# Softmax division of the second attention by 32 by 32 transposes, and the output projection issued one place earlier

## The chip, the cores and the metric

The kernel runs on one core of one Trainium2 chip. A core has TensorE (PE, matrix products), VectorE (DVE), ScalarE (ACT), GpSimd (POOL) and SyncE (SP, which only issues DMAs); each has a queue of its own that it works through in order, and they wait for each other by semaphores. Matrix products are written to PSUM (eight banks of 512 float32 columns on 128 partitions), the rest lives in SBUF. The metric is the device time in microseconds of one execution.

## The reference, cut to what matters

Two layers, each `x + attention(norm(x)) * silu(ffn(norm(x)))`, on 32 batches of 256 tokens with 128 channels (16 heads of 8). The change lies in the second layer's attention:

```python
q, k, v = xn @ q_w, xn @ k_w, xn @ v_w          # 16 heads of 8
scores = q @ k.T / sqrt(8)                      # q times sigmoid(unity_scale)
allowed = (j % 4 == 0) | (abs(i - j) <= 8)      # 64 strided keys and a band
attn = softmax(where(allowed, scores, -inf))
out = (attn @ v) @ o_w + o_b
x = x + out * silu(moe(xn))                     # 8 experts, top 2, capacity 2048
```

## The kernel before

The kernel goes through five stages: norm and projections, first attention with routing, first experts, end of layer 1, then the second attention with the second experts in its midst. The second attention works one batch of 256 tokens a step; `t` counts the steps in every engine's program. After step `MOE_AFTER` = 21 all engines run the second layer's experts, and steps 22 to 32 follow. From step 23 on, the steps also hold the final sums (`combine_last`, `gate_last` on VectorE, `tanh_last` on ScalarE, `sum_last` on GpSimd, loads and stores on SyncE), one group of 512 tokens in about every 0.6 steps.

The order of the work is written out by hand, in a loop over `t` in each engine's program. TensorE's step `t` is, in order:

1. first half of the maxima of batch t+1 (`maxima_pe`, lines 1779 and 1783: scores with queries on partitions, in banks 0 to 3),
2. weighing of the values, second half of the heads of batch t-1 (`weigh`, line 1845, into bank 6),
3. scores of batch t, first half of the heads (`second_scores`, line 1816) and the maximum subtracted (`less_maximum`, line 1826), banks 2 to 5,
4. keys of batch t+2 (`keys_second`, line 1743, bank 7),
5. second half of the maxima of batch t+1,
6. output projection of batch t-1 (`output_second`, line 1854, four products into bank 6),
7. values of batch t+1 (`values_second`, line 1753, bank 7),
8. weighing, first half of the heads of batch t; scores, second half; the maximum turned (`turn_max`, line 1799), queries of batch t+3 (line 1728).

The second half of the maxima writes banks that ScalarE's exponential (`exponents`, line 883) has to read first: it waits for the first of the two instructions of `exponents(t, 0)`. The first reduction of the maxima has to be done before the scores of the same half are written.

VectorE's step `t`: both reductions of the first maxima (`maxima_dve`, line 1355, 1024 columns each), the division of batch t-1 (`divide_second`), in late steps final sums (lines 1407, 1410, 1420), the result taken out of bank 6 with the bias added (`keep_second`, line 1396, which waits for the output projection), both reductions of the second maxima, and the maximum split into three bf16 parts (`split_max`, lines 1366 to 1372). TensorE's next weighing into bank 6 (item 8) waits for line 1396.

ScalarE's step: in the old kernel the masked copy `second_halves` (line 892) of bank 6, the exponentials, copies and masks of keys, queries and values.

What the division does: bank 6 holds, on the 32 partitions of each of four groups of heads, for heads 0 and 1 of the group the values on rows 0 to 15 and the sums of the exponentials on rows 16 to 31 (columns 0 to 255 are the queries), and for heads 2 and 3 (columns 256 to 511) the other way round. Before, the two column halves were mixed into DEN and NUM by two masks over partitions, with ScalarE's copy SEC of the masked half, DEN was moved by 16 partitions (`stream_shuffle`), inverted (256 columns) and multiplied with NUM.

The division of batch 21 and its projection lie in the experts' stage, behind the first transpose of rows and the first up-projection; the last division is at the very end, behind the last group's sums.

Of the kernel before, what the change touches and what calls it, by code (L numbers as in the profile page):

```python
# [8 lines left out]
ALU = mybir.AluOpType  # L9
# [3 lines left out]
P = 128  # L13
T = 8192
NT = T // P
NB = 32
# [149 lines left out]
def memory(nc, ctx, a, out):  # L166
# [50 lines left out]
    m.tix = small[:, 72:144]  # L217
    m.pcol = small[:, 144:145]
    m.eoff = small[:, 146:154]
    m.first_half, m.second_half = small[:, 158:159], small[:, 159:160]  # L220
    m.row = small[:, 160:302]
    m.mk = [small[:, 154 + j:155 + j] for j in range(4)]
    lg_words = m.LG[:].rearrange("p i e -> p (i e)")
# [105 lines left out]
    m.KS.append(sbx(bt, "KS2", [P, 576]))  # L329
    m.K4.append(sbx(bt, "K41", [P, 4, 320]))  # L330
    m.Q4.append(sbx(bt, "Q41", [P, 4, 256]))
    m.RC = sbx(bt, "RC", [P, 256])
    m.YC = sbx(bt, "YC", [P, 256])
    r.O = sbx(bt, "r1O", [P, 2, NT, E], BF16)
    r.O2 = r.O[:].rearrange("p k i e -> p (k i) e")
# [12 lines left out]
    x.W = [sbx(bt, f"W1_{k}", [P, 2, 512]) for k in range(2)]  # L348
    x.X = [sbx(bt, f"X1_{k}", [P, 2 * ROW]) for k in range(6)]
    m.b1s, m.b2s = sbx(bt, "b1s", [P, E, 4]), sbx(bt, "b2s", [P, E, C])  # L350
    m.SEC = sbx(bt, "SEC", [P, 512])
    m.DEN, m.NUM = sbx(bt, "DEN", [P, 256]), sbx(bt, "NUM", [P, 256])
    bt.close()

    xn_words = m.XNp[:].rearrange("p i c -> p (i c)")
# [28 lines left out]
def semaphores(nc, ctx):  # L384
    s = Sems()

    def sem(name):
        return ctx.enter_context(nc.semaphore(name))

    s.v_seq = sem("v_seq")  # L390

    s.const, s.upb, s.sw, s.zero, s.w0, s.c1, s.bb = (sem("l_" + n) for n in ("const", "upb", "sw", "zero", "w0", "c1", "bb"))
    s.zero_y, s.placed, s.to, s.nb, s.norm_a, s.norm_p, s.cnt_row = (sem(n) for n in (
        "l_zero_y", "placed", "to", "nb", "norm_a", "norm_p", "cnt_row"))

    s.wv0, s.vl, s.va, s.vd = (sem(n) for n in ("l_wv0", "vl", "va", "vd"))
    s.x = [sem(f"l_x{k}") for k in range(8)]
    s.scat0, s.scat1 = sem("l_scat0"), sem("l_scat1")

    s.zero_ready, s.var, s.rstd, s.norm, s.xpose, s.xt = (sem(n) for n in (  # L400
        "zero_ready", "var", "rstd", "norm", "xpose", "xt"))

    s.gate, s.gate_exp, s.onehot, s.cnt, s.cnt_sb, s.rank, s.total, s.total_sb, s.low, s.low_used, s.slots, s.ub = (
        sem(n) for n in ("gate", "gate_exp", "onehot", "cnt", "cnt_sb", "rank", "total", "total_sb", "low", "low_used",
                         "slots", "ub"))

    s.zvm, s.proj, s.rt, s.rq, s.ka, s.qm, s.vm, s.sc1, s.ev1, s.mask, s.sc2, s.prod, s.pv, s.yt = (sem(n) for n in (
        "zvm", "proj", "rt", "rq", "ka", "qm", "vm", "sc1", "ev1", "mask", "sc2", "prod", "pv", "yt"))

    s.at_row, s.xg, s.eup, s.eact, s.edown, s.y = (sem(n) for n in ("l_at_row", "xg", "eup", "eact", "edown", "y"))  # L410
    s.W = [[sem(f"l_W{n}_{k}") for k in range((5, 2)[n])] for n in range(2)]
    s.X = [[sem(f"l_X{n}_{k}") for k in range(6)] for n in range(2)]
    s.Y = [[sem(f"l_Y{n}_{k}") for k in range(4)] for n in range(2)]

    s.sup, s.hact, s.sdown = (sem(n) for n in ("sup", "hact", "sdown"))
    s.xb = [sem(f"l_xb{k}") for k in range(5)]
    s.yg = [sem(f"l_yg{k}") for k in range(3)]
    s.x1d = [sem(f"l_x1d{k}") for k in range(5)]
    s.comb, s.u, s.tanh, s.oproj, s.p6, s.x1, s.lg1, s.lg_sb = (sem(n) for n in (
        "comb", "u", "tanh", "oproj", "p6", "x1", "lg1", "lg_sb"))  # L420

    s.zw, s.zv, s.xw, s.qp, s.kp, s.vp, s.qs, s.ks, s.vn, s.q4, s.k4 = (sem(n) for n in (
        "zw", "zv", "xw", "qp", "kp", "vp", "qs", "ks", "vn", "q4", "k4"))
    s.scl_a, s.scl, s.max, s.maxv, s.neg, s.mturn, s.mvt = (sem(n) for n in (
        "scl_a", "scl", "max", "maxv", "neg", "mturn", "mvt"))
    s.sc, s.ex, s.wv, s.sec, s.yn, s.o1, s.given = (sem(n) for n in ("sc", "ex", "wv", "sec", "yn", "o1", "given"))
    s.zg = [sem(f"l_zg{k}") for k in range(NF)]
    s.zx = [sem(f"l_zx{k}") for k in range(NF)]
    s.out = [sem(f"l_out{k}") for k in range(NF)]
    s.fcomb, s.ftanh, s.taken, s.fex, s.fx = (sem(n) for n in ("fcomb", "ftanh", "taken", "fex", "fx"))  # L430
    return s
# [452 lines left out]
                     m.ps[:, (2 + 2 * half) * 512:(4 + 2 * half) * 512], ACT.Exp, scale=m.scl[:, 0:1]).then_inc(s.ex, 1)  # L884


def second_halves(e, m, s, b):

    e.wait_ge(s.wv, 2 * b + 2)
    if b >= 1:  # L890
        e.wait_ge(s.yn, b)
    e.mul(m.SEC[:], m.PS[6][:, 0:512], m.second_half).then_inc(s.sec, 1)


def expert_act(e, m, s, x, n, func, bias):
    if n == 0:
        e.wait_ge(s.ub, 1)
# [45 lines left out]
def scalar_program(e, m, s):  # L943
# [82 lines left out]
    for t in range(NB + 1):  # L1026
        if t == 2:
            e.wait_ge(s.gate, 2)
            e.activation(m.LG[:], m.LG[:], ACT.Exp).then_inc(s.gate_exp, 1)
        if t < 2:  # L1030
            end_act(e, m, s, NG - 2 + t, 1)
        if 1 <= t < NB and t - 1 != MOE_AFTER:
            second_halves(e, m, s, t - 1)
        if t < NB:
            exponents(e, m, s, t, 0)
        if t < 2:
            end_act(e, m, s, NG - 2 + t, 2)
        if t + 2 < NB:
            keys_copy(e, m, s, t + 2)
            keys_apart(e, m, s, t + 2)  # L1040
        if t + 1 < NB:
            value_pad(e, m, s, t + 1)
        for p in pairs_combined(t)[0]:
            tanh_last(e, m, s, p)
        if t + 1 < NB:
            queries_apart(e, m, s, t + 1, (0, 1))
        if t < NB:
            exponents(e, m, s, t, 1)
        if t + 1 < NB:
            queries_apart(e, m, s, t + 1, (2, 3))  # L1050
            maximum_copy(e, m, s, t + 1)
        if t + 3 < NB:
            queries_copy(e, m, s, t + 3)
        for p in pairs_combined(t)[1]:
            tanh_last(e, m, s, p)
        if t == NB:
            second_halves(e, m, s, NB - 1)
        if t == MOE_AFTER:
            second_halves(e, m, s, t)
            expert_act(e, m, s, m.x1, 1, ACT.Relu, lambda i, j: m.b1s[:, i // 8, j:j + 1])  # L1060


# [311 lines left out]

def divide_second(e, m, s, o, b):

    first, second = m.PS[6][:, 0:256], m.PS[6][:, 256:512]
    e.wait_ge(s.sec, b + 1)
    den = o.mark(e.scalar_tensor_tensor(m.DEN[:], second, m.first_half, m.SEC[:, 0:256], ALU.mult, ALU.add))
    o.mark(e.scalar_tensor_tensor(m.NUM[:], first, m.first_half, m.SEC[:, 256:512], ALU.mult, ALU.add))  # L1380
    o.wait(den)
    o.mark(e.stream_shuffle(m.RC[:], m.DEN[:], [i ^ 16 for i in range(32)]))
    o.wait()
    o.mark(e.reciprocal(m.RC[:], m.RC[:]))
    o.wait()
    if b >= 1:
        e.wait_ge(s.o1, b)
    e.tensor_tensor(m.YC[:], m.NUM[:], m.RC[:], ALU.mult).then_inc(s.yn, 1)


def keep_second(e, m, s, b):
# [559 lines left out]
def tensor_program(e, m, s):  # L1951
# [79 lines left out]
    for t in range(NB + 1):  # L2031
        if t == 0:
            turn_max(e, m, s, 0)
        if t + 1 < NB and t != MOE_AFTER + 1:
            maxima_pe(e, m, s, t + 1, 0)
        if t == MOE_AFTER + 1:
            e.wait_ge(s.y, NX0 + NX1)
        if t >= 1 and t - 1 != MOE_AFTER:
            weigh(e, m, s, t - 1, 1)
        if t in (0, 1, 6):  # L2040
            e.wait_ge(s.mvt, t + 1)
            e.wait_ge(s.qs, t + 3)
        if t < 2:
            end_pe(e, m, s, NG - 2 + t, 1)
        if t == 6:
            route_ranks(e, m, s, m.r1, 1, 0)
        if t < NB:
            second_scores(e, m, s, t, 0)
            less_maximum(e, m, s, t, 0)
        if t < 2:  # L2050
            end_pe(e, m, s, NG - 2 + t, 2)
        if t + 2 < NB:
            keys_second(e, m, s, t + 2)
        if t + 1 < NB:
            maxima_pe(e, m, s, t + 1, 1)
        if t >= 1 and t - 1 != MOE_AFTER:
            output_second(e, m, s, t - 1)
        if t + 1 < NB:
            values_second(e, m, s, t + 1)
        if t < NB:  # L2060
            weigh(e, m, s, t, 0)
            if t in (5, 6):
                e.wait_ge(s.vn, t + 2)
            if t == 5:
                route_counts(e, m, s, m.r1, 1)
            if t == 6:
                route_ranks(e, m, s, m.r1, 1, 1)
            second_scores(e, m, s, t, 1)
            less_maximum(e, m, s, t, 1)
        if t + 1 < NB:  # L2070
            turn_max(e, m, s, t + 1)
        if t + 3 < NB:
            queries_second(e, m, s, t + 3)
        if t == MOE_AFTER:
            weigh(e, m, s, t, 1)
            e.wait_ge(s.maxv, 4 * t + 8)
            e.wait_ge(s.ex, 4 * t + 4)
            expert_pe(e, m, s, m.x1, 1)
# [27 lines left out]
def _constants():  # L2106
# [11 lines left out]
    sm[:, 160:302] = np.arange(P)[:, None] + P * np.arange(142)[None, :]  # L2118
    for j in range(4):
        sm[:, 154 + j] = (np.arange(P) // 8) % 4 == j  # L2120
    sm[:, 158] = (np.arange(P) // 16) % 2 == 0
    sm[:, 159] = (np.arange(P) // 16) % 2 == 1
    c["c_small"] = sm
    c["c_tok"] = np.tile(NX1 * SL + np.arange(2 * NT, dtype=f) * P, (P, 1)).astype(f)
    inv = (f(1.0) / np.power(f(10000.0), np.arange(0, 8, 2, dtype=f) / f(8))).astype(f)
# [78 lines left out]
```

## Time and profile before

| | us |
|---|---|
| median of 3 runs | 1639.22 (1637.23 to 1644.84) |
| the profiled execution | 1639.27 |
| its span, first to last instruction | 1638.0 |
| mean granted TensorE clock | 0.991 of full speed |
| second attention, steps 0 to 21 | 950 to 1248 |
| second attention, steps 22 to 32 | 1478 to 1638 |

Busy time is counted per engine over the whole span. The chain of waits is followed back from the last instruction, at each step to what released it. In the timelines a number in brackets is the time that the engine idled before the row, with the engine and line that ended it; PEld is TensorE's weight load, which runs beside its products.

### The profile page before, as it was taken

How to read it: one execution, taken by the hardware profiler on the slowest of the kernel's cores; microseconds unless marked ns; L12 is line 12 of the kernel's file. 1: busy time of each engine (PE TensorE's matmuls, PEld its weight loads, DVE VectorE, ACT ScalarE, POOL GpSimd, SP SyncE). 2: the span in 40 equal slices, each digit the busy share in tenths (PEclk: the TensorE clock that was granted, in tenths of full speed). 3: DMA queues.
4: the chain of work that ended last, by engine and by line, in shares of the span. 5: the costliest groups of instructions: out<-in, count | busy, mean ns of one | idle time of the engine just before them, and what ended most of it. 6: DMA issues, size and time to landing. Idle time of an engine off the chain costs nothing.

```text
span 1638.0 us, 46884 instructions
## 1 busy us (share of the span) xinstructions
PE 1523.8 (93%) x18055; PEld 1110.6 (68%) x18059; DVE 1025.1 (63%) x2095; ACT 1007.8 (62%) x2071; POOL 830.5 (51%) x908
## 2 busy tenths in 40 slices
PE   7999999999999999999999989899998999999884
PEld 5555444555545889988777756666666999996553
DVE  6788898878775222212499969877775222226997
ACT  5767666777765444544545557777776455456773
POOL 7334587888874455545212210377774555552432
PEclk9999999999999999999999989999999999999998
DMA  9910002000004889888344310011113544433434
GB/s 313 417 56 1 8 31 100 29 28 30 30 29 85 229 216 245 230 216 235 91 117 120 85 55 3 16 50 44 47 45 60 95 89 101 90 70 97 117 100 117
DMA packets 296954, 169.45 MB, mean 103 GB/s; under 512 B 198080, under 2 KB 273216, under 8 KB 293792
## 3 DMA queue, kind: packets, MB, share of 16 engines
q1 hardware_dynamic: 277312, 128.45, 30.1%
q0 software_dynamic: 16832, 34.64, 6.1%
q10 hardware_dynamic: 2592, 3.38, 0.7%
q8 instruction: 147, 2.41, 0.6%
q14 instruction: 71, 0.58, 0.1%
HBM read 96.74 MB, written 69.63 MB: 102 GB/s over the span
## 4 chain that ended last, share of the span: by engine, by line
PE 59%; DVE 12%; issue 9%; POOL 9%; DMA 4%; ACT 4%; SPq 3%; DVEq 0%; POOLq 0%; ACTq 0%
PE ps L1884 12%; PE ps L1875 12%; PE ps L1688 6%; POOL xd L624 4%; DVE s_RS L1355 4%; PE ps L1916 4%; POOL s_S L657 4%; PE ps L1904 3%; PE ps L1779 3%; DMA s_W<-in_ew 3%; PE ps L1816 3%; ACT s_PX L883 3%; PE ps L1712 3%; PE ps L1652 2%; SPq L461 2%
## 5 line engine op out<-in xcount | busy, mean ns | idle before, releaser
L817 ACT ACTIVATE s_S<-ps 128x512 f32<-128x512 f32 x384 | 208.4, 595 | 141.4 <-PE ps L1688 141.4
L624 POOL DMA_INDIRECT xd<-s_XN,s_slots x256 | 251.2, 981 | 84.8 <-issue 62.2
L1542 DVE TENSOR_TENSOR s_PP<-ps,s_S 128x1024 f32<-128x1024 f32 x192 | 234.4, 1221 | 74.2 <-PE ps L1688 52.7
L1688 PE MATMUL ps<-s_QM,s_KK 32*128 32x512 f32 x1536 | 233.8, 639 | 2.7 <-ACT s_S L817 2.7
L906 ACT ACTIVATE s_HH<-ps,s_LG 128x256 f32<-128x256 f32 x284 | 125.2, 474 | 138.1 <-PE ps L1875 135.5
L641 POOL DMA_INDIRECT yd<-s_Y,s_to x142 | 136.0, 958 | 138.4 <-DVE s_Y L1484 114.3
L657 POOL TENSOR_SCALAR_AFFINE_SELECT s_S<-s_S 128x1024 f32<-128x1024 f32 x128 | 140.6, 1098 | 114.3 <-ACT s_S L817 113.7
L1355 DVE TENSOR_REDUCE s_RS<-ps 128x8 f32<-128x1024 f32 x128 | 150.3, 1216 | 62.0 <-PE ps L1783 62.0
L883 ACT ACTIVATE s_PX<-ps,s_scl 128x1024 f32<-128x1024 f32 x128 | 135.7, 1111 | 86.8 <-PE ps L1826 86.8
L906 ACT ACTIVATE s_XN<-ps,s_b1s 128x256 f32<-128x256 f32 x256 | 113.3, 474 | 113.9 <-PE ps L1875 110.6
L641 POOL DMA_INDIRECT yd<-s_XN,s_to x128 | 122.5, 957 | 117.0 <-DVE s_XN L1484 95.1
L1484 DVE TENSOR_TENSOR s_Y<-ps,s_W 128x256 f32<-128x256 f32 x71 | 30.1, 424 | 210.3 <-PE ps L1884 210.3
L1875 PE MATMUL ps<-s_XG,s_W 128*128 128x256 f32 x568 | 136.8, 384 | 13.3 <-DMA s_W<-in_ew 12.5
L1884 PEld LDWEIGHTS ps<-s_W,s_HH 128*128 128x128 f32 x1136 | 137.8, 192 | 3.6
L1884 PE MATMUL ps<-s_W,s_HH 128*128 128x128 f32 x1136 | 138.1, 275 | 0.0
L1484 DVE TENSOR_TENSOR s_XN<-ps,s_b2s 128x256 f32<-128x256 f32 x64 | 27.2, 424 | 171.5 <-PE ps L1884 171.5
L1712 PEld LDWEIGHTS ps<-s_PP,s_VM 128*32 128x32 f32 x3072 | 76.1, 109 | 84.8 <-DVE s_PP L1542 52.1
L1884 PEld LDWEIGHTS ps<-s_W,s_XN 128*128 128x128 f32 x1024 | 124.3, 192 | 3.3
L1875 PE MATMUL ps<-s_XN,s_W 128*128 128x256 f32 x512 | 122.9, 383 | 3.9 <-DVE s_XN L1471 3.0
L1884 PE MATMUL ps<-s_W,s_XN 128*128 128x128 f32 x1024 | 124.6, 275 | 0.0
L1875 PEld LDWEIGHTS ps<-s_XG,s_W 128*128 128x128 f32 x568 | 102.3, 190 | 28.2 <-DMA s_W<-in_ew 15.4
L795 ACT ACTIVATE s_QM<-s_RQ,s_small 128x256 f32<-128x256 f32 x252 | 113.9, 507 | 0.4 <-issue 0.4
(223 smaller groups left out, 2782.8 us busy)
## 6 DMA issues: line engine op xcount, KB each, us to landing
s_W<-in_ew SPq DMA_DIRECT2D x71, 576.0 KB, 4.6
s_X<-xd SPq DMA_DIRECT2D x540, 32.0 KB
xd<-s_zero SPq DMA_DIRECT2D x16, 1056.0 KB, 18.1
s_YG<-yd SPq DMA_DIRECT2D x32, 256.0 KB, 3.7
s_XN<-yd SPq DMA_DIRECT2D x32, 256.0 KB, 4.0
yd<-s_zero SPq DMA_DIRECT2D x7, 1056.0 KB, 27.9
s_XN<-in_x SPq DMA_DIRECT2D x8, 512.0 KB, 7.1
xd<-s_XN,s_slots POOLq DMA_INDIRECT x256
```

The costliest lines, as they stand in the source:

```text
L624: e.indirect_dma_start(out=xd, out_offset=bass.IndirectOffsetOnAxis(ap=m.slots[:, k, i:i + 1], axis=0), in_=m.XNp[:, i, 0:C + 1], in_offse ...
L641: e.indirect_dma_start(out=x.yd, out_offset=bass.IndirectOffsetOnAxis(ap=m.to[n][:, 2 * i + t:2 * i + t + 1], axis=0), in_=x.Y[i % 4][:, t ...
L657: e.affine_select(out=sel, in_=sel, pattern=[[0, 8], [1, P]], compare_op=ALU.is_ge, fill=0.0, base=0, channel_multiplier=-1).then_inc(s.ma ...
L817: e.mul(m.S1[u % 3][:, t * 512:(t + 1) * 512], m.PA[:, t * 512:(t + 1) * 512], 1.0 / 64.0).then_inc(s.ev1, 1)
L883: e.activation(m.PX[hp][:, 2 * half:2 * half + 2, :].rearrange("p r n -> p (r n)"), m.ps[:, (2 + 2 * half) * 512:(4 + 2 * half) * 512], AC ...
L906: e.activation(x.HH[i % 2][:, j, :], m.PS[j][:, 0:SL], func, bias=bias(i, j)).then_inc(s.eact, 1)
L1355: e.tensor_reduce(m.MM[b % 2][:, hf, 8 * rp:8 * rp + 8], m.ps[:, 1024 * rp:1024 * rp + 1024].rearrange("p (x n) -> p x n", x=8), AX.X, ALU ...
L1542: e.tensor_tensor(m.PP[u % 4][:], m.PB[u % 2], m.S1[u % 3][:], ALU.mult).then_inc(s.prod, 1)
L1688: return e.matmul(out, m.KK[k][32 * r:32 * r + 32, kind, kc * P:(kc + 1) * P], m.QM[k][32 * r:32 * r + 32, kind, :, qc * P:(qc + 1) * P], ...
L1712: i = e.matmul(m.PS[6][32 * c:32 * c + 32, qc * P:(qc + 1) * P], m.VM[b % 2][:, kc, 4 * c + h, :], m.PP[(2 * q + c // 2) % 4][:, (c % 2) * ...
L1875: e.matmul(PS[j][:, 0:SL], W[:, 0, j * P:(j + 1) * P], x.XG[i % 2][:], start=True, stop=True).then_inc(s.eup, 1)
L1884: ins = e.matmul(PS[4 + i % 2][:, c * P:(c + 1) * P], x.HH[i % 2][:, j, c * P:(c + 1) * P], W[:, 1, j * C:(j + 1) * C], start=(j == 0), st ...
```

## The change

VectorE transposes bank 6 (512 columns) in squares of 32 by 32 into TM, so that 32 queries lie on the partitions of a group and each head's sum is one column for 32 queries. It inverts 32 columns, multiplies twice (128 columns each, the inverse repeated 8 times) into YM and transposes YM (256 columns) back into YC. It waits for the weighing itself (`wv`) where it waited for ScalarE's copy (`sec`). The copy, its semaphore, the tensors SEC, DEN and NUM and the two masks are gone; the tensors are placed anew, RC has 32 columns. On TensorE `output_second(t - 1)` stands in front of `maxima_pe(t + 1, 1)`; in step 21's experts and in its own waits it is unchanged.

```diff
 def divide_second(e, m, s, o, b):
 
-    first, second = m.PS[6][:, 0:256], m.PS[6][:, 256:512]
-    e.wait_ge(s.sec, b + 1)
-    den = o.mark(e.scalar_tensor_tensor(m.DEN[:], second, m.first_half, m.SEC[:, 0:256], ALU.mult, ALU.add))
-    o.mark(e.scalar_tensor_tensor(m.NUM[:], first, m.first_half, m.SEC[:, 256:512], ALU.mult, ALU.add))
-    o.wait(den)
-    o.mark(e.stream_shuffle(m.RC[:], m.DEN[:], [i ^ 16 for i in range(32)]))
-    o.wait()
-    o.mark(e.reciprocal(m.RC[:], m.RC[:]))
-    o.wait()
+    e.wait_ge(s.wv, 2 * b + 2)
+    o.mark(e.transpose(m.TM[:], m.PS[6]))
+    o.wait()
+    o.mark(e.reciprocal(m.RC[:].rearrange("p (b h x) -> p b h x", b=8, h=2), view(m.TM[:], 16, [[32, 8], [240, 2], [8, 2]])))
+    o.wait()
+    for hp in range(2):
+        value = view(m.TM[:], 272 * hp, [[32, 8], [8, 2], [1, 8]])
+        one_over = view(m.RC[:], 2 * hp, [[4, 8], [1, 2], [0, 8]])
+        o.mark(e.tensor_tensor(view(m.YM[:], 16 * hp, [[32, 8], [8, 2], [1, 8]]), value, one_over, ALU.mult))
+    o.wait()
     if b >= 1:
         e.wait_ge(s.o1, b)
-    e.tensor_tensor(m.YC[:], m.NUM[:], m.RC[:], ALU.mult).then_inc(s.yn, 1)
+    e.transpose(m.YC[:], m.YM[:]).then_inc(s.yn, 1)
...
-def second_halves(e, m, s, b):
-
-    e.wait_ge(s.wv, 2 * b + 2)
-    if b >= 1:
-        e.wait_ge(s.yn, b)
-    e.mul(m.SEC[:], m.PS[6][:, 0:512], m.second_half).then_inc(s.sec, 1)
...
@@ scalar_program
-        if 1 <= t < NB and t - 1 != MOE_AFTER:
-            second_halves(e, m, s, t - 1)
...
-        if t == NB:
-            second_halves(e, m, s, NB - 1)
         if t == MOE_AFTER:
-            second_halves(e, m, s, t)
...
@@ tensor_program
             keys_second(e, m, s, t + 2)
+        if t >= 1 and t - 1 != MOE_AFTER:
+            output_second(e, m, s, t - 1)
         if t + 1 < NB:
             maxima_pe(e, m, s, t + 1, 1)
-        if t >= 1 and t - 1 != MOE_AFTER:
-            output_second(e, m, s, t - 1)
```

## Rows read from the trace of the kernel before

**Rows 1.** The page's busy time of each engine, share of the span, instructions.

```profile
PE 1523.8 (93%) x18055; PEld 1110.6 (68%) x18059; DVE 1025.1 (63%) x2095; ACT 1007.8 (62%) x2071; POOL 830.5 (51%) x908
```

**Rows 2.** Pieces of the chain of waits, steps 10, 11 and 15: start, us, what.

```profile
1094.27 1.12 ACT s_PX L883
...
1104.14 1.24 DVE s_RS L1355
...
1163.38 2.35 DVE s_RS L1355 x2
```

**Rows 3.** Timeline of step 10: start, us, engine, line, operation, shapes [idle before].

```profile
1089.55 1.12 PE L1779 MATMUL ps<-s_K,s_QS 32*64 32x512 f32 x16 [0.31 <-ACT s_PX L883]
...
1091.03 2.35 DVE L1355 TENSOR_REDUCE s_RS<-ps 128x8 f32<-128x1024 f32 x2 [2.62 <-PE ps L1783]
...
1093.33 0.48 DVE L1379 SCALAR_TENSOR_TENSOR s_DEN<-ps,s_small,s_SEC 128x256 f32<-128x256 f32 x1
...
1094.51 0.70 PE L1743 MATMUL ps<-s_XW,s_RS 128*128 128x320 f32 x2
...
1095.44 1.12 PE L1779 MATMUL ps<-s_K,s_QS 32*64 32x512 f32 x16 [0.23 <-ACT s_PX L883]
...
1096.38 0.43 DVE L1388 TENSOR_TENSOR s_YC<-s_NUM,s_RC 128x256 f32<-128x256 f32 x1
...
1096.93 0.64 PE L1854 MATMUL ps<-s_RS,s_YC 128*128 128x128 f32 x4
...
1097.41 1.06 PE L1753 MATMUL ps<-s_RS,s_XW 128*128 128x128 f32 x8
1097.61 0.42 DVE L1396 TENSOR_TENSOR s_RS<-ps,s_RS 128x256 f32<-128x256 f32 x1 [0.80 <-PE ps L1854]
1097.96 1.21 DVE L1355 TENSOR_REDUCE s_RS<-ps 128x8 f32<-128x1024 f32 x1
```

**Rows 4.** Durations by line on VectorE, ns: min/median/max, first and last start.

```profile
L1384 DVE RECIPROCAL s_RC<-s_RC x32: 1752/1753/1754, 971.3 to 1631.3; 128x256 f32<-128x256 f32 x32
...
L1246 DVE RECIPROCAL s_mx<-s_mx x1: 553/553/553, 993.0 to 993.0; 128x64 f32<-128x64 f32 x1
...
L1471 DVE STREAM_TRANSPOSE s_XN<-s_X x64: 403/434/446, 1250.7 to 1471.3; 128x256 f32<-128x256 f32 x64
...
L1447 DVE TENSOR_TENSOR s_XN<-s_XN x1: 691/691/691, 1629.4 to 1629.4; 128x512 f32<-128x512 f32 x1
...
L1368 DVE TENSOR_TENSOR s_RS<-s_RS x32: 191/193/633, 946.9 to 1606.7; 128x32 f32<-128x32 f32 x32
```

**Rows 5.** Waits, 950 to 1250 us: total us, times, longest.

```profile
PE ps L1816 <- DVE s_RS L1355: 8.1, 21, 1.3
...
PE ps L1799 <- DVE s_RS L1372: 1.2, 3, 0.5
```

**Rows 6.** Who waited for line 1355, 1055 to 1240 us: total us, times.

```profile
  PE ps L1816: 3.7, 14
```

**Rows 7.** Timeline of TensorE in step 24.

```profile
1515.91 1.10 PE L1845 MATMUL ps<-s_PX,s_VN 128*32 128x64 f32 x64 [1.25 <-DVE s_RS L1396]
```

**Rows 8.** Who waited for line 1396, whole span: total us, times.

```profile
  PE ps L1845: 8.8, 9
```

**Rows 9.** Chain of waits, first reductions of steps 23 and 30, first and last of eight.

```profile
1493.35 2.35 DVE s_RS L1355 x2
...
1595.75 2.27 DVE s_RS L1355 x2
```

**Rows 10.** Timeline of step 31 and the end.

```profile
1609.49 1.10 PE L1845 MATMUL ps<-s_PX,s_VN 128*32 128x64 f32 x64 [1.66 <-ACT s_PX L883]
...
1611.38 0.48 DVE L1379 SCALAR_TENSOR_TENSOR s_DEN<-ps,s_small,s_SEC 128x256 f32<-128x256 f32 x1 [3.46 <-ACT s_SEC L892]
...
1622.16 3.91 DVE L1407 TENSOR_SCALAR s_XN<-s_XN,s_wgt 128x128 f32<-128x128 f32 x4
...
1633.55 1.22 PE L1854 MATMUL ps<-s_RS,s_YC 128*128 128x128 f32 x4 [9.69 <-DVE s_YC L1388]
```

More of the change, by code:

```diff
@@ L219, in memory @@
     m.eoff = small[:, 146:154]
-    m.first_half, m.second_half = small[:, 158:159], small[:, 159:160]
     m.row = small[:, 160:302]
@@ L331, in memory @@
     m.Q4.append(sbx(bt, "Q41", [P, 4, 256]))
-    m.RC = sbx(bt, "RC", [P, 256])
+    m.YM = sbx(bt, "YM", [P, 256])
     m.YC = sbx(bt, "YC", [P, 256])
@@ L350, in memory @@
     m.b1s, m.b2s = sbx(bt, "b1s", [P, E, 4]), sbx(bt, "b2s", [P, E, C])
-    m.SEC = sbx(bt, "SEC", [P, 512])
-    m.DEN, m.NUM = sbx(bt, "DEN", [P, 256]), sbx(bt, "NUM", [P, 256])
+    m.TM = sbx(bt, "TM", [P, 512])
+    m.RC = sbx(bt, "RC", [P, 32])
     bt.close()
@@ L425, in semaphores @@
         "scl_a", "scl", "max", "maxv", "neg", "mturn", "mvt"))
-    s.sc, s.ex, s.wv, s.sec, s.yn, s.o1, s.given = (sem(n) for n in ("sc", "ex", "wv", "sec", "yn", "o1", "given"))
+    s.sc, s.ex, s.wv, s.yn, s.o1, s.given = (sem(n) for n in ("sc", "ex", "wv", "yn", "o1", "given"))
     s.zg = [sem(f"l_zg{k}") for k in range(NF)]
@@ L2120, in _constants @@
         sm[:, 154 + j] = (np.arange(P) // 8) % 4 == j
-    sm[:, 158] = (np.arange(P) // 16) % 2 == 0
-    sm[:, 159] = (np.arange(P) // 16) % 2 == 1
     c["c_small"] = sm
```

## The prediction

> **What bounds the kernel now.** I read the busy table first: TensorE works 93% of the span, VectorE 63% [rows 1], so VectorE's saved time is worth something only where it ends a wait. The diff touches the second attention, 32 batches: steps 0 to 21 lie at 950 to 1248 us, steps 22 to 32 at 1478 to 1638 us, the second experts between. I then read the chain of waits there. In a usual step it runs through TensorE, with ScalarE's first exponential as one link: 1094.27 + 1.12 ends at X = 1095.39, and TensorE goes on 0.05 later [rows 2]. VectorE stands in it for one reduction. Steps 1 to 21 each hold an output projection. In 8 of these 21 the chain passes through both reductions of the second group (2.35 us together [rows 2]), so VectorE's queue sets the pace. The other 13 are TensorE's. I call them V-steps (8) and T-steps (13).
>
> The timeline of one T-step [rows 3] shows where the division lies. VectorE's reductions end at R = 1093.38; five instructions follow, from 1093.33 to 1096.81 (the last starts at 1096.38, 0.43 long): 3.48 us. TensorE meanwhile does the keys (to 1095.21), waits 0.23 for X, does the second maxima from 1095.44, the output projection from 1096.93, the values from 1097.41. The division is done before its consumer's turn. VectorE then waits 0.80 us for the projection before line 1396, and only after that reduces the second group, at 1097.96 = X + 2.57.
>
> **The division, step by step.** Reciprocal costs 1.753 us for 256 columns and 0.553 for 64 [rows 4], 6.25 ns a column, so 32 columns take 0.553 - 0.200 = 0.35. A transpose of 256 columns takes 0.434, an elementwise one of 256 0.42 [rows 3, 4], of 512 0.69, of 32 0.19 [rows 4], about 1.04 ns a column over 0.16. So the transpose of 512 is 0.70, the two products of 128 columns are 0.29 each, and the second starts some 0.08 before the first ends, as lines 1379 and 1380 overlap in the trace (0.50 for both), the last transpose 0.43. With three hand-overs of 0.04: 0.70 + 0.04 + 0.35 + 0.04 + 0.50 + 0.04 + 0.43 = 2.10, against 3.48: 1.38 less.
> No row shows a transpose of 512 columns out of PSUM. Below it cannot be under 0.43 (256 columns), above I take the 1.21 of a reduction of 1024 PSUM columns [rows 3]. The reciprocal of 32 lies between 0.19 (another operation of 32) and 0.55, the products between 0.19 and 0.42 each. Together the chain is between 1.6 and 3.2; I take 2.10, since the nearest rows lie on one line.
> The Trainium skill, "VectorE: DVE Perf Modes", section on the TRN2 errata, adds 62 cycles at 0.96 GHz to an operation whose source is in PSUM. The trace has 0.42 for line 1396 (PSUM) and 0.43 for line 1388 (SBUF) [rows 3], so it does not bear this out. By the rule the chain would be 2.16 and the estimate below some 2 us higher.
>
> **ScalarE's masked copy** (L892) leaves, 0.69 us in each batch. It was hidden: in the steps it runs while VectorE reduces and ends before R. It counted only in step 31, where VectorE waited 3.46 for it [rows 10]: the weighing there ends at 1610.59, the division starts at 1611.38, 0.79 later; 0.05 will do, so 0.74 goes.
>
> **The projection in front.** It now stands behind the keys and waits for the division; the second maxima, values, weighing and scores queue behind it. The division ends at 1093.33 + 2.10 = 1095.43, or X + 0.04. Then 0.05 of latency, 0.1 for a weight load that nothing hides now, and 0.46 for its four products: the maxima start at X + 0.65 instead of X + 0.05. The maxima need 1.49 until the next operation starts (1095.44 to 1096.93), so the values start at X + 2.14 instead of 1097.41 = X + 2.02. With the cold start of the maxima I take 0.15 of loss in a T-step. If the division ended before 1095.2 the projection would lie wholly in the hole and a T-step would gain up to 0.2.
> In T-steps: 13 x 0.15 = 1.95 us slower.
> In V-steps the reductions no longer wait for the projection and line 1396. They start when the first maxima banks are done, 1.48 after the maxima begin (1089.55 to 1091.03 in the other half of this step), at X + 2.13 instead of X + 2.57: 0.4 earlier on VectorE's side, 0.15 later on TensorE's [rows 3]. What can be won is how long TensorE waited more than in a T-step. It waited 8.1 us in 21 waits for the first reduction [rows 5] where 3.7 us in 14 are usual (0.264 each) [rows 6], so 2.5 over, and 1.2 for the split maximum [rows 5]: 3.7 in 8 steps. Each gives back at most 0.4, less the 0.15: some 1.8 in all.
> The two cancel: steps 1 to 21 come out at 0, and the experts' stage too, where the projection stands behind the first up-projection and the division fits beside it.
>
> **Steps 23 to 30.** Here VectorE also does the final sums, ahead of line 1396. Step 24 shows it: the weighing behind line 1396 starts at 1515.91 after 1.25 us of idle TensorE [rows 7]; nine such waits make 8.8 us [rows 8]. The division sits in front of all that, so its 1.38 comes off directly until TensorE is the limit again: a T-step lasts 13.1 (first reductions at 1091.03 [rows 3] and 1104.14 [rows 2]; over the T-steps the mean is 13.05), with the loss 13.2 us. The first reductions of the eight steps start between 1493.35 and 1595.7 [rows 9]; the seven steps between them are 13.90, 15.04, 14.76, 13.91, 14.68, 13.90 and 16.13 us. The three near 13.9 fall to 13.2 (0.70 each), the four others by 1.38, and the last by 1.3: 2.1 + 5.5 + 1.3 = 8.9 us.
>
> **Step 31 and the end.** In step 31 the masked copy and the division lie open: 0.74 + 1.38 = 2.1. VectorE's queue is then unbroken from line 1396 to the last division, with one slow group (3.91 us for four instructions [rows 10]). The last division starts at 1630.03, long after its weighing, and the projection waits for it until 1633.55 [rows 10]: 1.4 more.
>
> Sum: 0 + 8.9 + 2.1 + 1.4 = 12.4 us. The profiled execution took 1639.27 us (span 1638.0), within 0.1 of the median, so the forecast is 1627.
>
> **Rivals.** With the chain at 2.10 + d, about 31 places pay d (21 steps, 8 in the tail, 2 at the end), so the time is 1627 + 31 d and no gain is left at d = 0.40.
> A, slower: the projection blocks TensorE's queue. If the transpose out of PSUM needs twice the 0.70, d is 0.7, the maxima start at X + 1.35 in every step, and the sum is -12.4 + 21.7 = +9.3: 1648.6. For it: nothing in the trace shows this operation, and the wait is new. Against: all VectorE rows on PSUM go at the pace of those on SBUF. Chance 0.10.
> B, little gain: in the tail VectorE and GpSimd get in each other's way. Four instructions of line 1407 took 3.91 us beside GpSimd's sums, and 0.87 elsewhere, 3.0 more [rows 10]. If moving the queue makes two more such meetings, or TensorE takes more than 0.15 for the new order (0.3 in 28 steps costs 4 more), the time is 1632 to 1635. Chance 0.20. The Trainium skill, "SBUF — State Buffer", section "SBUF: two separate sides", calls the port pair of the two engines an exclusive lock that also VectorE instructions with two SBUF inputs ask for; the new products are such, as the old one was.
> C, more gain: the division is 0.25 shorter, the projection falls into the hole behind the keys. T-steps then give 0.2 instead of taking 0.15 (13 x 0.35 = 4.6), V-steps and tail some 3: 1620. Chance 0.13.
> My forecast, 1622 to 1631: 0.55. The remaining 0.02 is for what I have not seen.
>
> **Range and chances.** The bounds of the chain give 1616 (d = -0.5, where the hole caps the gain) to 1660 (d = 1.1); 80% is 1619 to 1639. What a measurement here can tell from no change is about 0.5%, 8.2 us: under 1631 counts as faster, over 1647.4 as slower. Faster 0.71 (forecast, C, a little of B), same 0.20, slower 0.09.
>
> **What would show it.** The division from its first transpose to its last: 2.1 us, the first 0.70, the reciprocal 0.35. The projection starts about 0.05 after the last transpose and within 0.2 of X. TensorE's wait for line 1396 goes from 8.8 us to under 1. T-steps stay within 0.3 of 13.05. Steps 23 to 30 shrink by 0.7 to 1.4 each. A projection that waits more than 0.5 behind the keys, or T-steps above 13.4, would make the prediction wrong; so would tail steps that don't shrink.

## The result, and the profile after

The changed kernel takes 1637.87 us (median of 20 runs, 1632.88 to 1642.11); the kernel before, run beside it, 1642.21 us (20 runs). The ratio is 0.9972 with a 95% interval of 0.9962 to 0.9983: faster by 0.28%, 4 to 5 us, where 12.4 us were forecast. That lies within the 0.5% that the prediction takes for no change, and outside its 1622 to 1631.

The page's busy row of the changed kernel, as [rows 1]:

```profile
PE 1530.1 (94%) x18055; PEld 1116.5 (68%) x18059; DVE 986.2 (60%) x2063; ACT 986.5 (60%) x2039; POOL 832.0 (51%) x908
```

VectorE gave up 38.9 us, ScalarE 21.3 us (32 masked copies), and the span shrank by 2.1 us (1635.9 after 1638.0). TensorE does the same 18055 instructions and is busy 6.3 us longer. That says little by itself, since its mean granted clock was 0.988 here and 0.991 before.

The timeline of step 9 of the new kernel around its division, first VectorE, then TensorE, to be read against [rows 3] (start, us, engine, line, operation; in brackets the idle time before and what ended it):

```profile
1080.33 2.36 DVE L1341 TENSOR_REDUCE s_RS<-ps 128x8 f32<-128x1024 f32 x2 [3.50 <-PE ps L1770]
1082.61 0.70 DVE L1364 STREAM_TRANSPOSE s_TM<-ps 128x512 f32<-128x512 f32 x1
1083.34 0.35 DVE L1366 RECIPROCAL s_RC<-s_TM 128x32 f32<-128x32 f32 x1
1083.73 0.49 DVE L1371 TENSOR_TENSOR s_YM<-s_TM,s_RC 128x128 f32<-128x128 f32 x2
1084.26 0.45 DVE L1375 STREAM_TRANSPOSE s_YC<-s_YM 128x256 f32<-128x256 f32 x1
1085.51 0.42 DVE L1383 TENSOR_TENSOR s_RS<-ps,s_RS 128x256 f32<-128x256 f32 x1 [0.80 <-PE ps L1841]
1086.88 2.36 DVE L1341 TENSOR_REDUCE s_RS<-ps 128x8 f32<-128x1024 f32 x2 [0.94 <-PE ps L1770]
```

```profile
1083.81 0.70 PE L1730 MATMUL ps<-s_XW,s_RS 128*128 128x320 f32 x2
1084.76 0.71 PE L1841 MATMUL ps<-s_RS,s_YC 128*128 128x128 f32 x4 [0.25 <-DVE s_YC L1375]
1085.40 1.11 PE L1766 MATMUL ps<-s_K,s_QS 32*64 32x512 f32 x16
1086.45 0.61 PE L1770 MATMUL ps<-s_RS,s_identb 128*128 128x256 bf16 x4
1086.89 1.06 PE L1740 MATMUL ps<-s_RS,s_XW 128*128 128x128 f32 x8
1087.88 1.20 PE L1832 MATMUL ps<-s_PX,s_VN 128*32 128x64 f32 x64
1089.01 0.72 PE L1803 MATMUL ps<-s_Q,s_KS 32*128 32x128 f32 x14
1090.14 0.93 PE L1803 MATMUL ps<-s_Q,s_KS 32*128 32x128 f32 x18 [0.41 <-issue]
1091.01 1.05 PE L1813 MATMUL ps<-s_RS,s_AUG 128*128 128x256 bf16 x8
```

The division runs from 1082.61 to 1084.71: 2.10 us, as forecast. The projection starts 0.05 later and the second maxima 0.64 after it. In the last row but one TensorE stops for 0.41 in the middle of its 32 score products, and no semaphore ends that. The bracket understates it: from the first score product to the next group it takes 2.00 us (1089.01 to 1091.01), in a step without a stop 1.11. The kernel before has no such stop of over 0.15 us in its second attention.

The wait of [rows 8] in the new kernel (who waited for line 1383, whole span: total us, times), and the new kernel's rows of step 31 and the end, as [rows 10]:

```profile
  PE ps L1832: 0.2, 1
```

```profile
1610.63 1.10 PE L1832 MATMUL ps<-s_PX,s_VN 128*32 128x64 f32 x64 [1.66 <-ACT s_PX L882]
...
1611.80 0.72 DVE L1364 STREAM_TRANSPOSE s_TM<-ps 128x512 f32<-128x512 f32 x1 [2.74 <-PE ps L1832]
...
1621.70 3.61 DVE L1394 TENSOR_SCALAR s_XN<-s_XN,s_wgt 128x128 f32<-128x128 f32 x4 [0.22 <-DMA s_XN<-yd]
...
1631.42 1.22 PE L1841 MATMUL ps<-s_RS,s_YC 128*128 128x128 f32 x4 [7.78 <-DVE s_YC L1375]
```

To see where the gain went I measured distances between the starts of the maxima groups on TensorE (line 1779 before, 1766 after). Half a step lies between two of them. Two halves are one step. An ordinary step is the length of the steps that nothing else disturbs. "Steps 2-21" runs from the first maxima of step 2 to the second maxima of step 21, "experts" from there to the first maxima of step 22, "steps 22-29" from there to those of step 30. For all kernels of one chip, in us, from their profiled executions:

| kernel | ordinary step | steps 2-21 | experts | steps 22-29 | the rest |
|---|---|---|---|---|---|
| before | 13.02 | 258.7 | 238.4 | 114.7 | 45.5 |
| changed | 13.19 | 263.8 | 238.9 | 110.5 | 40.6 |
| division only (e1) | 12.97 | 257.7 | 239.3 | 108.1 | 40.7 |
| move only (e2) | 14.56 | 289.6 | 238.0 | 118.6 | 47.6 |
| division between (e3) | 12.78 | 259.8 | 238.5 | 112.6 | 41.4 |

"The rest" runs from step 30 to the end of the span. The changed kernel wins 9.1 us in the last two columns and loses 5.1 in steps 2 to 21; 1.8 more are lost at the beginning and in the experts, of which 1.1 lie ahead of the second attention. Of the 5.1, 0.7 is the measuring point: the second maxima of step 21 now stand behind the projection. From the first maxima of step 2 to those of step 21 the loss is 4.5 us.

The time up to step 2 isn't in the table. It is 980.8, 982.1, 987.7, 981.1 and 988.2 us in the order of the rows. The profiled execution of e1 took 4.8 us more than the median of its kernel, that of e3 3.2 more, and it is in this part that they are long. So the columns are compared one by one, and whole times by medians.

### The profile page after: what moved, and what is told of

It reads as the page before. It is cut to its first block, busy times and chain, and to the rows that moved or that the text cites. A ratio compares the mean times of both kernels' runs of the same rounds, so it can differ in the third digit from the quotient of the medians.

```text
span 1635.9 us, 46789 instructions
## 1 busy us (share of the span) xinstructions
PE 1530.1 (94%) x18055; PEld 1116.5 (68%) x18059; DVE 986.2 (60%) x2063; ACT 986.5 (60%) x2039; POOL 832.0 (51%) x908
## 4 chain that ended last, share of the span: by engine, by line
PE 62%; DVE 11%; POOL 9%; issue 8%; DMA 4%; ACT 3%; SPq 2%; POOLq 0%; DVEq 0%; ACTq 0%
PE ps L1871 13%; PE ps L1862 13%; PE ps L1675 6%; DVE s_RS L1341 4%; POOL xd L623 4%; PE ps L1766 4%; POOL s_S L656 4%; PE ps L1903 4%; PE ps L1891 3%; PE ps L1699 3%; PE ps L1639 2%; DMA s_W<-in_ew 2%; PE ps L1803 2%; PE ps L1832 2%; ACT s_PX L882 2%
## 5 line engine op out<-in xcount | busy, mean ns | idle before, releaser
L897 ACT ACTIVATE s_XN<-ps,s_b1s 128x256 f32<-128x256 f32 x256 | 113.3, 474 | 115.4 <-PE ps L1862 111.2
```

Of the source, the lines that this page charges most:

```text
L897: e.activation(x.HH[i % 2][:, j, :], m.PS[j][:, 0:SL], func, bias=bias(i, j)).then_inc(s.eact, 1)
```

## The experiments

**The changed kernel again (e0).** No edit. 

> The changed kernel once more, nothing altered. Theory O (order): the projection in front of the second maxima costs 0.2 us in every step where TensorE sets the pace, so such a step lasts 13.2 to 13.25 us again (before: 13.05). Theory S (stalls): in the first trace TensorE stood still seven times for 0.2 to 0.9 us in the midst of a row of equal products, with nothing waited for (3.1 us in all, none in the kernel before); if these belong to the new order they come back at about the same places, if they are an accident of the execution they come back elsewhere or not at all. Time as measured, 0.996 to 0.999 of the kernel before.

Measured: 1638.37 us, ratio 0.9975 (0.9961 to 0.999). TensorE's stops, told of below, come back in the same steps (at 998.10, 1081.57, 1095.08, 1188.96, 1559.75, 1586.44 and 1592.64 us, and a small one at 1101.78), though this execution runs some 5 us later. They belong to the program and not to chance, though two of them differ in length (0.17 and 0.76 in the first execution, 0.72 and 0.22 here).

**The division alone (e1).** TensorE in its old order:

```diff
-        if t >= 1 and t - 1 != MOE_AFTER:
-            output_second(e, m, s, t - 1)
         if t + 1 < NB:
             maxima_pe(e, m, s, t + 1, 1)
+        if t >= 1 and t - 1 != MOE_AFTER:
+            output_second(e, m, s, t - 1)
```

> The new division with the projection left behind the second maxima. Theory O: steps 1 to 21 go at 13.05 us again, the steps 23 to 30 fall as far as 13.05 instead of 13.2, the end gains the same 4.8 us (masked copy and two open divisions): 9 to 14 us under the kernel before, 5 us or more under the changed kernel. Rival, stalls alone (S as an accident): the order costs nothing, this kernel is within 2 us of the changed one, and its ordinary steps are no shorter. Rival, the prediction's V-steps: the earlier projection was worth 1.8 us in the eight steps that VectorE paces, which this kernel gives up, so those steps are as long as before.

Measured: 1629.96 us, ratio 0.9917 (0.9901 to 0.9934), 13.9 us under the kernel before and 8.4 under the changed one. It beats both. Its timeline of TensorE in a usual step:

```profile
1087.68 0.70 PE L1730 MATMUL ps<-s_XW,s_RS 128*128 128x320 f32 x2
1088.61 1.12 PE L1766 MATMUL ps<-s_K,s_QS 32*64 32x512 f32 x16 [0.23 <-ACT s_PX L882]
...
1090.11 0.61 PE L1841 MATMUL ps<-s_RS,s_YC 128*128 128x128 f32 x4
```

The division of this step ends at 1088.58 and the projection uses it at 1090.11. In the old order the short division has 1.5 us to spare, and the hole behind the keys (0.23) stays with the exponential. Who waited for line 1383 in this kernel:

```profile
  PE ps L1832: 2.0, 1
```

Nine waits of 8.8 us [rows 8] became one of 2.0, without any move on TensorE. By the columns of the table the move costs 6.1 us in steps 2 to 21, 2.4 in steps 22 to 29 and nothing behind them.

**The move alone (e2).** The old division and masked copy, TensorE in the new order; the edit is against the kernel before:

```diff
+        if t >= 1 and t - 1 != MOE_AFTER:
+            output_second(e, m, s, t - 1)
         if t + 1 < NB:
             maxima_pe(e, m, s, t + 1, 1)
-        if t >= 1 and t - 1 != MOE_AFTER:
-            output_second(e, m, s, t - 1)
```

> The old division with the projection moved in front. Theory O: the old division ends 1.42 after ScalarE's first exponential (X), so the second maxima start at X + 2.05 instead of X + 0.05 and each step of 1 to 21 grows by 1.5 us, in the tail by 0.6 to 1.5: 30 to 45 us slower than before, 1.020 to 1.027. Rival (TensorE's queue is not blocked by the wait): within 5 us of the kernel before.

Measured: 1679.46 us, ratio 1.023 (1.0209 to 1.0251). One step of its TensorE:

```profile
1092.08 0.70 PE L1743 MATMUL ps<-s_XW,s_RS 128*128 128x320 f32 x2
1094.45 0.71 PE L1854 MATMUL ps<-s_RS,s_YC 128*128 128x128 f32 x4 [1.67 <-DVE s_YC L1388]
1095.10 1.11 PE L1779 MATMUL ps<-s_K,s_QS 32*64 32x512 f32 x16
```

In this order the division is on the path in every step: 1.38 us more of it, 1.37 more per step (14.56 after 13.19). So rival A's mechanism is real, and only the shortness of the new division kept it out. TensorE's stops are here too: three in the late steps, 1.4 us together.

**The division between the two reductions (e3).** On VectorE, everything else as in the changed kernel:

```diff
-            maxima_dve(e, m, s, t + 1, 0)
+            maxima_dve(e, m, s, t + 1, 0, (1,) if between else (1, 0))
...
+        if between:
+            maxima_dve(e, m, s, t + 1, 0, (0,))
```

> The changed kernel with the division placed between the two reductions of the first maxima on VectorE. It then ends 1.2 us earlier, before the keys are done; the second reduction ends at X + 0.1 instead of X - 2.0. Theory O: the projection fills the hole between the keys and the second maxima, these start at X + 0.15 to X + 0.35 (changed kernel: X + 0.72), a step of 1 to 21 lasts 12.8 to 12.95, and the time is 8 to 15 us under the changed kernel, 0.988 to 0.993 of the kernel before. Rival: the second maxima now wait for the late second reduction as long as they waited for the projection, and the time is that of the changed kernel within 3 us.

Measured: 1638.49 us, ratio 0.997 (0.9954 to 0.9985). The shortest steps fall to 12.78, the lowest of all: the division is done earlier, and TensorE takes the projection right behind the keys, while it would wait for the exponential. But few steps are that short. From step 8 to 20 the median is 13.10 (13.22 in the changed kernel, 13.00 in e1). The stops have become more (nine over 0.15 us, 4.6 us together), seven times the second maxima wait for the late second reduction instead (2.3 us), and the time is that of the changed kernel. So both the expectation's theory and its rival show, the rival in a minority of steps. One of them stands inside the 64 weighing products:

```profile
1203.74 1.09 PE L1835 MATMUL ps<-s_PX,s_VN 128*32 128x64 f32 x63
1205.60 0.22 PE L1835 MATMUL ps<-s_PX,s_VN 128*32 128x64 f32 x1 [0.76 <-issue]
```

**The stops.** These rows of TensorE in the changed kernel have idle time in the middle of a group that nothing releases:

```profile
993.11 0.73 PE L1803 MATMUL ps<-s_Q,s_KS 32*128 32x128 f32 x16 [0.24 <-issue]
...
1552.32 0.70 PE L1813 MATMUL ps<-s_RS,s_AUG 128*128 128x256 bf16 x5 [0.91 <-issue]
...
1585.21 0.27 PE L1832 MATMUL ps<-s_PX,s_VN 128*32 128x64 f32 x2 [0.76 <-issue]
```

The DMA view of the changed kernel from 1087 to 1090.2 us (queue, kind: packets, MB, share of 16 engines) has one transfer of instructions ahead of the stop that ends at 1090.14:

```profile
q8 instruction: 1, 0.02, 2.6%
```

By the record it is 16 KB, starts at 1087.49 and takes 1.35, so it lands 1.30 us before TensorE goes on. All the other stops end 1.26 to 1.48 us after such a packet has landed, too. There are 147 packets on this queue in the span. My reading is that TensorE had used up its instructions and the next block came late. No run shows that directly: there is no row for the engine's wait. Two theories on why the new order has such stops: (position) where the ends of the blocks fall among the groups decides it, and any edit shifts them; (order) the new order itself makes the fetch late. 64 or 128 waits that are already satisfied, in front of TensorE's first work, shift all that follows:

```diff
+    for _ in range(128):
+        e.wait_ge(s.zero_ready, 1)
```

**The changed kernel shifted by 64 and 128 (e4, e5), the division alone and the division between shifted by 128 (e6, e7).** 

> The changed kernel with 64 waits on a semaphore that is long set, put into TensorE's program at its very start, so that all its later instructions lie 64 places further on in the instruction stream. In the changed kernel every unexplained stop of TensorE ends 1.2 to 1.5 us after a 16 KB packet of its instruction queue has landed, and both runs have them in the same steps. Theory B (blocks): a stop comes where the end of a 16 KB block falls into a dense row of products in an unlucky place; shifted, the stops go from steps 10, 17 and 27 to others or vanish; the time may move some us either way. Rival (the stops belong to those steps of the work, whatever the instructions' place): stops in the same steps as before, same time as the changed kernel plus at most 2 us for the waits.

> The same with 128 waits, half a block. Theory B: stops in other steps than in the changed kernel and in the kernel with 64; their sum over steps 2 to 21 (3.2 us there) may be anything from 0 to 8. Rival: the same steps. In ordinary steps without a stop both theories have 13.2 us, since the order of the projection is unchanged.

> The new division with the projection in its old place, shifted by 128. Without a shift it had no stop at all. Theory B: that was luck of the place, with the shift some steps get stops and it loses 1 to 5 us on the unshifted one; ordinary steps stay at 13.0. Rival (the old order is not open to such stops, because TensorE waits for the exponential in front of the long dense part): no stops again, 1630 us within 3.

> The division between the two reductions, projection in front, shifted by 128. Unshifted, its steps without a stop last 12.8 us, but many have one, hidden or open, and it was no faster than the changed kernel. Theory B: with the stops elsewhere the time differs from the unshifted one by several us, to below 1630 if few are left. Rival: within 2 us of the unshifted one.

Measured, against a kernel before that took 1703.99 us on this chip: 1692.34 (ratio 0.9932, 0.9906 to 0.9959), 1691.68 (0.9934, 0.9915 to 0.9953), 1693.49 (0.9945, 0.9922 to 0.9968) and 1692.61 (0.9932, 0.9909 to 0.9955). The four can't be told apart. Here steps 7 to 21 last 15 to 20 us in every kernel instead of some 13.2, so most of what the set was to compare is covered by something else (last section). What can still be read: the step with the stop of 993.11 lasted 13.71 us, and lasts 13.29 and 13.19 with the shifts; in the late steps the stops lie at other places (1.66 and 1.45 us in e4, 1.15, 0.33 and 0.33 in e5). That speaks for position. In the same steps e7 has stops of 1.97, 0.93 and 0.45, and e6, in the old order, one of 0.39. So the question was left whether the order matters as well.

**Both orders, shifted and not, on one chip (f0 to f3).** f0 is the changed kernel, f1 the same with 128 waits, f2 the division alone, f3 the same with 128 waits.

> The changed kernel once more, as the base of this set. Steps 2 to 21 against the kernel before +4 to +6 us, ordinary scatter step about 13.2, TensorE stops at the scores of step 3 and around steps 9 to 11 and late in the tail; about 0.25% under the kernel before. Every theory expects this.

> The changed kernel with 128 already satisfied waits in front of TensorE's first work, so the same instructions lie 128 places further in its stream. Theory B (the stops come where the stream crosses the end of a fetched block, whatever the order is): the stops of step 3 and of steps 9 to 11 move or vanish, steps 2 to 21 come out up to 3 us shorter than in the unchanged one, ordinary step stays 13.2; time 0.1 to 0.3% under the unchanged one less the cost of the 128 waits. Rival (the order of the work makes the stops): same steps, same lengths, 1638.

> The new division with the old order on TensorE, as in the earlier set. Both theories: 1630, 0.8% under the kernel before, ordinary step 12.97, no stops of TensorE above 0.15 us between two rows of the same group.

> The new division with the old order and the 128 waits. Theory B (position alone): stops of 0.2 to 0.9 us appear in some steps, as they do in the changed kernel, and the time rises by 1 to 5 us to 1631 to 1635. Rival (order alone): no stops, 1630 as without the waits.

Measured, beside a kernel before of 1642.75 us:

| kernel | us | ratio (95%) | steps 2-21 | steps 22-29 | stops over 0.15 us behind a packet |
|---|---|---|---|---|---|
| f0 changed | 1636.99 | 0.9966 (0.995 to 0.9983) | 263.6 | 110.3 | 5, 1.9 us |
| f1 changed, shifted | 1636.82 | 0.9966 (0.9945 to 0.9987) | 262.4 | 113.3 | 6, 4.3 us |
| f2 division only | 1631.46 | 0.993 (0.9909 to 0.9951) | 257.9 | 107.7 | 0 |
| f3 division only, shifted | 1634.51 | 0.9954 (0.9934 to 0.9975) | 257.5 | 111.2 | 1, 0.3 us |

The shifted changed kernel's longest stop, from f1's timeline of TensorE:

```profile
1540.09 0.71 PE L1803 MATMUL ps<-s_Q,s_KS 32*128 32x128 f32 x11 [1.69 <-issue]
```

Neither theory alone holds. Position decides where: the stop of 993.11, in step 2, is gone (13.18 instead of 13.71), others lie elsewhere, and one of 1.69 is new. But steps 2 to 21 win only 1.3 where up to 3 were allowed, and 3.0 are lost in steps 22 to 29. And the count goes with the order: 7, 8 and 5 stops in three executions of the changed kernel and 6 in the shifted one, against 0 and 0 in the division alone and 1 in the shifted one; the kernel before has 0, and the move alone 3. So far as these few positions of each order tell, the new order brings them. The fetches show a trace of it. The seven blocks that land ahead of the changed kernel's stops are fetched 49 to 173 TensorE instructions later in the stream than the blocks of the same number in e1. In the second attention of the kernel before, e1, f2 and f3, a fetch starts seven to nine times while TensorE works on the keys; in the changed kernel, f0 and f1 never (in e0 once), and the blocks ahead of the stops start during or behind the values. Why the order moves the fetch stays open.

f3's tail is 3.4 us longer than f2's, and that looks like the position theory's 1 to 5 us, but the rows say otherwise. VectorE of f3, then of f2, then TensorE of f3 and of f2 in that step:

```profile
1530.03 1.43 DVE L1394 TENSOR_SCALAR s_XN<-s_XN,s_wgt 128x128 f32<-128x128 f32 x4 [1.69 <-DMA s_XN<-yd]
...
1532.42 0.41 DVE L1383 TENSOR_TENSOR s_RS<-ps,s_RS 128x256 f32<-128x256 f32 x1
```

```profile
1532.05 0.88 DVE L1394 TENSOR_SCALAR s_XN<-s_XN,s_wgt 128x128 f32<-128x128 f32 x4 [0.49 <-DMA s_XN<-yd]
...
1534.28 0.41 DVE L1383 TENSOR_TENSOR s_RS<-ps,s_RS 128x256 f32<-128x256 f32 x1
```

```profile
1532.98 1.93 PE L1832 MATMUL ps<-s_PX,s_VN 128*32 128x64 f32 x64 [3.20 <-DVE s_RS L1383]
1534.84 2.09 PE L1803 MATMUL ps<-s_Q,s_KS 32*128 32x128 f32 x32
```

```profile
1534.83 1.10 PE L1832 MATMUL ps<-s_PX,s_VN 128*32 128x64 f32 x64 [1.89 <-DVE s_RS L1383]
1536.08 1.17 PE L1803 MATMUL ps<-s_Q,s_KS 32*128 32x128 f32 x32
```

In f3 VectorE waits 1.69 for the final sums' load, TensorE idles 3.20 behind it, and its clock falls (the windows view of f3 from 1533 to 1535 us; the third number from the end is the granted clock, 0.50, and it is 0.50 from 1535 to 1537 too):

```profile
1533.00:1535.00 2.00, 2.00 (x68) 1.83 (x68) 2.00 (x2) 0.96 (x3) 0.00 (x0) 0.50 0.37 112
```

So f3's loss is a late load and the clock behind it: 1.3 us more idle, and 0.83 in the weighing and 0.92 in the scores. These two rows and the idle time make 3.1 of the 3.3 us by which this step is longer. One execution shows that; whether the load is late in every run of f3 isn't known. The two profiled executions took the same time (1634.70 and 1634.68 us), since f2's was slower up to step 2, so the 3.1 us between the medians aren't explained by this for certain.

## Why the prediction was wrong in size

**The division: right.** Transpose 0.70, reciprocal 0.35, products 0.49 (0.50 forecast), second transpose 0.45 (0.43), 2.10 in all. The durations by line in the changed kernel (ns: min/median/max):

```profile
L1364 DVE STREAM_TRANSPOSE s_TM<-ps x32: 673/706/717, 970.5 to 1629.3; 128x512 f32<-128x512 f32 x32
...
L1366 DVE RECIPROCAL s_RC<-s_TM x32: 352/353/355, 971.3 to 1630.0; 128x32 f32<-128x32 f32 x32
```

A transpose out of PSUM goes at the pace that the rows from SBUF gave. The Trainium skill's "VectorE: DVE Perf Modes", section on the TRN2 errata, would have it some 0.06 longer; 0.706 against the 0.70 of the straight line does not bear it out.

**The ordinary T-step: right.** 13.19 instead of 13.02, 0.17 where 0.15 was forecast; the projection started 0.05 after the division, and it waited 0.25 behind the keys. 13 x 0.17 = 2.2 us lost, if every T-step paid it.

**The V-steps: right in direction, a third of the size.** The forecast let the reductions start 0.4 earlier and give 1.8 us back in eight steps, net 0.23 each. In the six of them without a stop the change is -0.19, -0.14, +0.06, +0.05, -0.23 and 0.00 (steps 3 to 6, 15 and 20): 0.45 back where 1.35 were forecast. Step 6 shows why it can fail, first the changed kernel's VectorE, then its TensorE:

```profile
1040.36 0.68 DVE L1133 TENSOR_TENSOR s_RS<-s_r1O,ps 128x512 f32<-128x512 bf16 x1
1040.96 0.71 DVE L1364 STREAM_TRANSPOSE s_TM<-ps 128x512 f32<-128x512 f32 x1
...
1042.61 0.45 DVE L1375 STREAM_TRANSPOSE s_YC<-s_YM 128x256 f32<-128x256 f32 x1
...
1045.23 2.36 DVE L1341 TENSOR_REDUCE s_RS<-ps 128x8 f32<-128x1024 f32 x2 [0.94 <-PE ps L1770]
```

```profile
1043.11 0.71 PE L1841 MATMUL ps<-s_RS,s_YC 128*128 128x128 f32 x4 [0.79 <-DVE s_YC L1375]
1043.76 1.11 PE L1766 MATMUL ps<-s_K,s_QS 32*64 32x512 f32 x16
...
1047.80 1.17 PE L1803 MATMUL ps<-s_Q,s_KS 32*128 32x128 f32 x32
```

TensorE of the kernel before, at the same scores:

```profile
1046.01 1.17 PE L1816 MATMUL ps<-s_Q,s_KS 32*128 32x128 f32 x32
```

Against the start of the exponential (1041.39 after, 1039.74 before) the second reductions do start 0.41 earlier (3.84 us behind it instead of 4.25). But in this V-step VectorE has other work (line 1133, the routing) in front of the division. There the projection waits 0.79 for the division, and the second maxima, values and weighing queue behind it: the maxima start 2.37 us behind the exponential instead of 1.17. The scores that need both then start 6.41 behind it instead of 6.27. The bound passed from VectorE to TensorE. I had priced TensorE's side with the T-step's 0.15, in just those steps where VectorE is late. The division alone took 0.54 off this step (14.48 in e1 after 15.02), and the move gave it back (15.07).

**The stops: not in the forecast at all.** Five of the steps 2 to 21 have one (steps 2, 8, 9, 10 and 16; step 10 shows it only in e0) and last 13.38 to 14.17. In steps 26 to 29 three more show 1.8 us.

Together these make the +4.5 of steps 2 to 20 where 0 was forecast: +1.1 in the eight T-steps without a stop, -0.45 in the six V-steps without one, +3.8 in the five with one. At 0.17 for the order in each of these five, some 2.9 are left for the stops.

**Steps 23 to 30: half right.** The wait for line 1396 fell from 8.8 us to 0.2, as forecast. The seven steps from 23 on gained 4.3 us by TensorE's maxima; five of them shrank by 0.7 to 1.3, two grew by 0.2 and 0.3. In e1 they gain 6.6. The difference is the order's: 0.2 a step and the stops. The forecast measured from VectorE's first reductions, and by these the seven steps gained 5.7 us (102.3 before, 96.6 after) where 7.6 were forecast.

**Step 31 and the end: right in its parts.** From the first maxima of step 30 to the end 4.8 us were won, as 1.3 + 2.1 + 1.4 = 4.8 were forecast. That they agree is in part luck: from the first reduction of step 30, which is what the forecast counted from, 3.4 were won, because this reduction waited longer for its turn before (3.1 us behind its maxima, 1.6 after) and the difference fell to the steps ahead of it. Either way the late steps and the end won 9.1 us of the 12.4. The division starts 0.07 behind the weighing (0.79 before), the last projection 2.15 behind the last division's start (3.52 before).

**The step that failed.** The term for the order: I put the move's loss at 13 x 0.15, took 1.8 of it back in V-steps, and counted the tail's gain as one of both edits. In place of "steps 1 to 21 come out at 0" the runs show 4.5 us of loss, as the V-steps gave back 0.45 in six and the stops took some 2.9; in place of 8.9 + 2.1 + 1.4 in the late steps they show 9.1. The division alone gives 13.9 us on one chip and 11.3 on the other, about my whole sum of 12.4; the move takes 8.4 and 5.5 of it away (e1 against e0, f2 against f0). The tail's gain needed no move, since there the division's 1.38 comes off VectorE's queue in either order.

**The rivals.** B named the outcome (TensorE takes more than 0.15 for the new order) but its time, 1632 to 1635, fell short of the measured 1637.87, because it knew of no stops. Its other half, VectorE and GpSimd in each other's way, is seen in f2: while GpSimd sums, one product of the division takes 1.36 us instead of 0.29. First GpSimd, then VectorE of f2:

```profile
1528.94 1.41 POOL L1419 TENSOR_TENSOR s_XN<-s_XN 128x512 f32<-128x512 f32 x1
```

```profile
1529.15 1.36 DVE L1371 TENSOR_TENSOR s_YM<-s_TM,s_RC 128x128 f32<-128x128 f32 x1
```

The product ends 0.16 us after GpSimd's sum does. The Trainium skill, "SBUF — State Buffer", section "SBUF: two separate sides", has both ask for one exclusive port pair; this row agrees, but such meetings are rare: in the changed kernel no product took more than 0.55. A came about only with the old division (e2). C did not come, as the division ends 0.2 us after the keys. But its hole is there: in e3 the projection fits into it, and the shortest steps are 12.78, C's 0.2 under 13.02; the stops and the waits for the late reduction ate it.

## What to carry to other kernels

Where one edit shortens a chain and another moves its consumer earlier, price each alone against the same rows: here the first made the consumer's operand ready 1.5 us ahead in an ordinary step, and the second only put the wait back at the head of TensorE's queue. An operation that waits belongs behind those that don't, above all in the steps in which its producer is late, and those are the steps from which the gain was expected. And when an in-order engine's stream is rearranged, look for idle time in the middle of a group that nothing releases, before the sum is trusted to 0.3%.

## What the runs showed of the hardware

TensorE stops in the middle of a group for 0.2 to 1.7 us and goes on 1.2 to 1.6 us after a 16 KB packet of its instruction queue has landed. Of the seven stops of one execution of the changed kernel the second (e0) has all, the third (f0) five. With 42 such packets in steps 2 to 21, only a few cost anything. If my reading of them as late instructions holds, instruction loading costs this kernel 3 to 5 of its 1638 us, which I did not expect.

After 3.20 us of idle TensorE the next groups ran at half clock (0.50, that is 1.2 GHz: weighing 1.93 instead of 1.10 us), after 1.89 us they did not (1.10), in the same step of two kernels that differ only in the 128 waits (f3 and f2, one execution each).

On the chip of the second set the kernel before took some 61 us more than on the others. The four kernels traced there take 54 to 64 us more than the same orders without the waits on the first chip, and most of that lies in the steps with GpSimd's scatter, 7 to 21 (steps 2 to 21 take 307.3 us in e5, 263.8 in the changed kernel), with stops of TensorE in the weighing such as this of e5:

```profile
1137.42 0.37 PE L1832 MATMUL ps<-s_PX,s_VN 128*32 128x64 f32 x8 [0.42 <-issue]
```

What is different there wasn't tried.
